# A graph layer's turn table: attention 21 turns sooner, 256-node blocks from node 4096

## The reference

```
msg = relu(x[src] + edge_attr @ w_e + b_e)                # gather of 131072 rows
agg = segment_sum(msg, dst, 8192)
h_local = bn1(relu((x + agg) @ w1 + b1) @ w2 + b2 + x)
q, k, v = split(x.reshape(256, 32, 256) @ in_w.T + in_b)  # attention inside 32 nodes, 4 heads
h_attn = bn2(softmax(q k^T / 8) v @ out_w.T + out_b + x)
out = h_local + h_attn
out = bn3(out + relu(out @ m_w1 + m_b1) @ m_w2 + m_b2)
return layernorm(x + out)
```

## Time and profile before

| | us |
|---|---|
| median of 3 runs | 1297.24 (1296.2 to 1297.25) |
| the profiled execution | 1296.03 |
| its span, first to last instruction | 1294.2 |
| busy: PE / DVE / ACT / POOL | 1154.5 / 826.7 / 541.2 / 944.9 |
| mean granted TensorE clock | 0.969 of full speed |

### The profile page before, as it was taken

The page is one execution under the profiler, slowest core; times in us unless marked ns, Lnnn a source line. Parts: engine busy times, 40 slices in busy tenths (PEclk is TensorE's granted clock), DMA queues, the critical chain, the costliest instruction groups (busy, mean ns, idle before and its releaser), DMA issues.

```text
span 1294.2 us, 28246 instructions
## 1 busy us (share of the span) xinstructions
PE 1154.5 (89%) x7309; PEld 647.4 (50%) x7309; DVE 826.7 (64%) x2090; ACT 541.2 (42%) x1077; POOL 944.9 (73%) x1004
## 2 busy tenths in 40 slices
PE   6787989998899899998989999998989998998896
PEld 3444454544445444444544545454444555765675
DVE  5847486767566576755758666575756667557563
ACT  1343434444344435434344443443434443443353
POOL 7777777777777777777777777777777777675770
PEclk7898999999999999999999999999999998999999
DMA  8554555655555555565555555555655565554550
GB/s 316 154 170 141 175 156 175 174 173 180 170 165 169 164 182 172 160 183 148 183 173 175 165 165 176 166 175 174 172 164 154 183 183 147 168 160 126 175 155 26
DMA packets 119282, 216.50 MB, mean 167 GB/s; under 512 B 24784, under 2 KB 69584, under 8 KB 119120
## 3 DMA queue, kind: packets, MB, share of 16 engines
q0 software_dynamic: 47808, 130.61, 35.0%
q1 hardware_dynamic: 67312, 79.47, 19.6%
q10 hardware_dynamic: 4000, 4.61, 1.0%
HBM read 197.82 MB, written 16.78 MB: 166 GB/s over the span
## 4 chain that ended last, share of the span: by engine, by line
PE 58%; DVE 11%; ACTq 8%; ACT 7%; issue 7%; POOL 6%; DMA 2%; DVEq 0%; SPq 0%
PE bank L837 33%; PE bank L867 12%; PE bank L882 7%; POOL xg L430 6%; ACTq L463 6%; ACT msg L469 4%; DVE bank L681 3%; PE bank L891 3%; ACTq L311 2%; DVE dif L731 2%; DVE mx L726 2%; PE bank L938 1%; DMA xT<-in_xT_dram 1%; DVE aggT L714 1%; ACT kbd L490 1%
## 5 line engine op out<-in xcount | busy, mean ns | idle before, releaser
L430 POOL DMA_INDIRECT xg<-in_x_dram,srcs x996 | 944.0, 948 | 317.4 <-issue 290.0
L469 ACT ACTIVATE msg<-bank 128x512 f32<-128x512 f32 x512 | 277.8, 595 | 543.6 <-PE bank L867 286.7
L681 DVE TENSOR_TENSOR bank<-xg,bank 128x512 f32<-128x512 f32 x498 | 327.4, 690 | 138.1 <-DMA xg<-in_x_dram,srcs 93.0
L867 PE MATMUL bank<-we,ea 64*128 64x256 f32 x2048 | 301.7, 415 | 35.5 <-DVE bank L681 35.5
L867 PEld LDWEIGHTS bank<-we,ea 64*128 64x128 f32 x2048 | 183.1, 192 | 179.7 <-issue 124.1
L714 DVE TENSOR_TENSOR aggT<-bank,aggT 128x64 f32 x512 | 115.2, 225 | 169.1 <-PE bank L891 115.2
L882 PE MATMUL bank<-msg,onehot 128*32 128x256 f32 x2048 | 141.1, 394 | 49.0 <-ACT msg L469 48.4
L837 PE MATMUL bank<-xT,iwT 128*128 128x512 f32 x256 | 128.2, 624 | 7.6 <-DMA xT<-in_xT_dram 4.0
L837 PE MATMUL bank<-o,m 128*128 128x512 f32 (+2 forms) x352 | 125.6, 491 | 4.6 <-DVE o L758 4.4
L882 PEld LDWEIGHTS bank<-msg,onehot 128*32 128x32 f32 x2048 | 54.4, 111 | 141.6 <-ACT msg L469 96.9
L837 PE MATMUL bank<-h,m 128*128 128x512 f32 (+2 forms) x352 | 116.6, 479 | 2.1 <-ACT h L529 2.1
(11 more groups left out here) (92 smaller groups left out, 938.9 us busy)
## 6 DMA issues: line engine op xcount, KB each, us to landing
rows<-in_x_dram SPq DMA_DIRECT2D x2304, 1.0 KB
ea<-in_ea_dram SPq DMA_DIRECT2D x128, 256.0 KB
rows<-in_x_dram ACTq DMA_DIRECT2D x1280, 1.0 KB
xg<-in_x_dram,srcs POOLq DMA_INDIRECT x996
xT<-in_xT_dram SPq DMA_DIRECT2D x32, 256.0 KB, 4.2
aggT<-in_xT_dram SPq DMA_DIRECT2D x32, 256.0 KB, 4.0
oT_dram<-oT SPq DMA_DIRECT2D x32, 256.0 KB
xn<-in_x_dram SPq DMA_DIRECT2D x32, 256.0 KB
```

Of the source, the lines that this page charges most:

```text
L430: pool.indirect_dma_start(xg[:, slot % NX, n * C:(n + 1) * C], None, t["x"], bass.IndirectOffsetOnAxis(k.srcs[:, at:at + 1], 0)).then_inc( ...
L469: nc.scalar.activation(msg[:, q % NM, :], EA[q % 4][:, :], ACT.Relu).then_inc(s_msg, 1)
L681: nc.vector.tensor_tensor(EA[q % 4][:, :].rearrange("p (a c) -> p a c", a=2), pair.rearrange("p (a c) -> p a c", a=2), KB[:, 0:C].unsqueez ...
L867: ins = nc.tensor.matmul(EA[(2 * d + pair) % 4][:, two * C:(two + 1) * C], ea[rows, n % NEA, at:at + P], k.we[rows, :], start=False, stop= ...
```

## The change

Attention starts its slabs at turns 0, 7, 14, 21 with a plan of seven turns, and from slab 4 at 16 J - 33 with a wider plan; before, it was 12 J for the first slabs and then 16 J - 12. `xT` has four slots instead of three, `oT` three instead of two, and the messages have four slots instead of eight. Blocks of 512 nodes end at node 4096 instead of 6144; fourteen blocks of 256 follow instead of six. SyncE loads x for the attention at other turns. From turn 254 on TensorE's order is written out by hand, and the attention's half of step B of the last two 128-node blocks becomes a step of its own, "A".

```
--- before.py
+++ after.py
@@ -26,7 +26,7 @@
 ND = NP // 2
 NB = N // IT
 NX = 7
-NM = 8
+NM = 4
 NEA = 3
 AHEAD = 3
 SLACK = 1
@@ -45,7 +45,7 @@
     0, 6, 8, 10, 12, 14, 16, 18, 20, 24, 26, 28)
 NV = 30
 
-NXT, NOT = 3, 2
+NXT, NOT = 4, 3
 
 ROWS, LOADED = 2 * P, 16
 SP_ROWS, SP_TURNS, SP_LEAD = 9, 242, 9
@@ -53,33 +53,36 @@
 SCALE_TURN, FOLD_TURN, BIAS_TURN = 9, 11, 12
 
 
-HEADS = {"q": (0, 1), "k": (2, 3), "sc": (4, 6), "soft": (5, 7), "v": (8, 9), "av": (11, 13)}
-HEADS_EARLY = {"q": (0, 1), "k": (2, 3), "sc": (4, 5), "soft": (5, 6), "v": (7, 8), "av": (9, 10)}
+HEADS = {"q": (0, 2), "k": (3, 5), "sc": (6, 8), "soft": (7, 9), "v": (10, 11), "av": (13, 14)}
+HEADS_EARLY = {"q": (0, 0), "k": (1, 1), "sc": (2, 3), "soft": (3, 4), "v": (4, 4), "av": (5, 6)}
+EARLY = 4
 
 
 def heads_base(J):
-    return max(16 * J - 12, 12 * J)
-
-
-
-BLOCKS = [(FULL * J, FULL) for J in range(12)] + [
-    (6144 + 256 * n, 256) for n in range(6)] + [(7680 + 128 * n, 128) for n in range(4)]
+    return 7 * J if J < EARLY else 16 * J - 33
+
+
+
+BLOCKS = [(FULL * J, FULL) for J in range(8)] + [
+    (4096 + 256 * n, 256) for n in range(14)] + [(7680 + 128 * n, 128) for n in range(4)]
 NODES = {"w1": (0, 1), "B": (3, 5), "z": (4, 6), "m1": (7, 8, 9, 10), "m2": (11, 13),
          "T": (14, 15), "log": (15, 16), "y": (16, 17), "xn": (8, 9), "out": (17, 18)}
 NODES_256 = {"w1": (0,), "B": (1,), "z": (2,), "m1": (2, 3), "m2": (4,), "T": (5,), "log": (6,),
              "y": (7,), "xn": (2,), "out": (8,)}
-FIRST_256 = {12: 211, 13: 217, 14: 223, 15: 229, 16: 235, 17: 243}
+FIRST_256 = dict(enumerate(
+    (147, 154, 161, 168, 175, 182, 189, 196, 203, 211, 219, 227, 235, 243), 8))
 NODES_128 = {
-    18: {"w1": (247,), "B": (248,), "z": (249,), "m1": (249,), "m2": (250,), "T": (251,),
+    22: {"w1": (247,), "B": (248,), "z": (249,), "m1": (249,), "m2": (250,), "T": (251,),
          "log": (252,), "y": (253,), "xn": (247,), "out": (254,)},
-    19: {"w1": (250,), "B": (251,), "z": (252,), "m1": (252,), "m2": (253,), "T": (254,),
-         "log": (255,), "y": (256,), "xn": (), "out": (257,)},
-    20: {"w1": (254,), "B": (255,), "z": (256,), "m1": (256,), "m2": (257,), "T": (258,),
-         "log": (259,), "y": (260,), "xn": (252,), "out": (261,)},
-    21: {"w1": (256,), "B": (257,), "z": (258,), "m1": (258,), "m2": (259,), "T": (260,),
-         "log": (260,), "y": (261,), "xn": (), "out": (262,)},
+    23: {"w1": (250,), "B": (251,), "z": (252,), "m1": (252,), "m2": (253,), "T": (254,),
+         "log": (256,), "y": (257,), "xn": (), "out": (258,)},
+    24: {"w1": (255,), "B": (256,), "z": (256,), "m1": (257,), "m2": (258,), "T": (260,),
+         "log": (260,), "y": (261,), "xn": (252,), "out": (262,)},
+    25: {"w1": (256,), "B": (257,), "z": (257,), "m1": (258,), "m2": (259,), "T": (260,),
+         "log": (260,), "y": (262,), "xn": (), "out": (263,)},
 }
-LASTB = 21
+LAST_TURN = 254
+LASTB = 25
 
 
 SUMS = {2 * n + 1: n for n in range(NG)}
...
...
...
@@ -366,10 +369,10 @@
                     load_ea(turn // 2 + 2)
                 if p == 3 and i + AHEAD < IT:
                     preload(i + AHEAD)
-                if turn in (2, 12):
-                    load_xT(1 if turn == 2 else 2)
-                if turn % 16 == 13 and NXT <= (turn + 19) // 16 < NJ:
-                    load_xT((turn + 19) // 16)
+                if turn in (1, 7, 13):
+                    load_xT((turn + 5) // 6)
+                if turn % 16 == 10 and NXT <= (turn + 38) // 16 < NJ:
+                    load_xT((turn + 38) // 16)
                 for J, _, pair in heads_in(turn - 1, ("av",)):
                     sp.wait_ge(s_oc, 2 * J + pair + 1)
                     sp.dma_start(k.oT_dram[2 * J + pair, :, :, :],
...
@@ -969,7 +972,7 @@
 
             def node(b, stage, use):
                 n0, w = BLOCKS[b]
-                at, to = cols(b), bank(b, stage)
+                at, to = cols(b), bank(b, "B" if stage == "A" else stage)
                 J, of_slab = part(b)
                 if stage == "w1":
                     if use:
@@ -978,9 +981,9 @@
                         if b == 0:
                             pe.wait_ge(s_w1, 16)
                             pe.wait_ge(s_bias, 1)
-                        elif b < 18:
+                        elif b < 22:
                             pe.wait_ge(s_r, before(b, "T"))
-                        elif b == 18:
+                        elif b == 22:
                             pe.wait_ge(s_oc, 2 * NJ)
                         elif b < LASTB:
                             pe.wait_ge(s_r, before(b - 1, "T"))
@@ -989,18 +992,21 @@
                         ins = product(to[:, of], CC, lambda a: k.w1[:, a, c * P:(c + 1) * P],
                                       lambda a: aggT[:, a, n0:n0 + w])
                     ins.then_inc(s_p1, 1)
+                if stage == "A":
+                    pe.wait_ge(s_oc, 2 * NJ)
+                    if b < LASTB:
+                        pe.wait_ge(s_h1, before(b + 1, "w1"))
+                    for c, of in chunks(b, "B", use):
+                        product(bank(b, "B")[:, of], CC,
+                                lambda a: k.owT[:, a, c * P:(c + 1) * P],
+                                lambda a: k.oT[:, J % NOT, a, of_slab], start=c == 0,
+                                stop=False, skip=True)
                 if stage == "B":
-                    early = b == LASTB
+                    early = b >= 24
                     if use:
                         pe.wait_ge(s_o, before(b, "B") + use)
                     else:
                         pe.wait_ge(s_oc, (n0 + w + NB - 1) // NB)
-                    if early:
-                        for c, of in chunks(b, "B", use):
-                            product(to[:, of], CC, lambda a: k.owT[:, a, c * P:(c + 1) * P],
-                                    lambda a: k.oT[:, J % NOT, a, of_slab], start=c == 0,
-                                    stop=False, skip=True)
-                    if not use:
                         pe.wait_ge(s_h1, before(b + 1, "w1"))
                     for c, of in chunks(b, "B", use):
                         if not early:
@@ -1039,9 +1045,8 @@
                                                       k.z[:, c, row:row + P], ident[:, :])
                     ins.then_inc(s_t, 1)
 
-            for turn in range(TURNS):
-                if turn < ND:
-                    products(turn)
+            for turn in range(LAST_TURN):
+                products(turn)
                 if turn - 1 in SUMS:
                     transpose_agg(SUMS[turn - 1])
                 weights(turn)
@@ -1051,6 +1056,25 @@
                     node(b, stage, use)
                 if turn in SUMS:
                     sum_group(SUMS[turn])
+
+            products(ND - 2)
+            transpose_agg(NG - 2)
+            node(23, "T", 0)
+            products(ND - 1)
+            node(24, "w1", 0)
+            sum_group(NG - 1)
+            node(24, "A", 0)
+            transpose_agg(NG - 1)
+            node(24, "B", 0)
+            node(LASTB, "A", 0)
+            node(LASTB, "w1", 0)
+            node(24, "m1", 0)
+            node(LASTB, "B", 0)
+            node(LASTB, "m1", 0)
+            node(24, "m2", 0)
+            node(LASTB, "m2", 0)
+            node(24, "T", 0)
+            node(LASTB, "T", 0)
             with pe.If(pe.value_load(k.bad_i[0:1, 0:1], min_val=0, max_val=1) > 0):
                 pe.wait_ge(s_go, 1)
                 general_tensor(nc, k, g, pe)
```

More of the change, by code:

```diff
@@ L127, in nodes_in @@
     for b in range(len(BLOCKS)):
-        if b < 12:
+        if b < 8:
             plan, base = NODES, 16 * b + 19
-        elif b < 18:
+        elif b < 22:
             plan, base = NODES_256, FIRST_256[b]
@@ L140, in heads_in @@
     for J in range(NJ):
-        plan = HEADS_EARLY if J < 3 else HEADS
+        plan = HEADS_EARLY if J < EARLY else HEADS
         found += [(J, s, n) for s in stages for n, at in enumerate(plan[s])
@@ L297, in bank @@
                 return EA[("w1", "B", "m1", "m2", "T").index(stage) % 4]
-            return k.XA if b in (18, 20) else k.XN
+            return k.XA if b in (22, 24) else k.XN
         x_bytes = t["x"].rearrange("(a n) c -> a (n c)", a=1).bitcast(u8)
@@ L401, in stored @@
                 for n in range(NOT):
-                    sp.wait_ge(s_ost[n], 16 * (IT // NOT))
+                    sp.wait_ge(s_ost[n], 32 * len(range(n, NJ, NOT)))
             with sp.If(sp.value_load(k.bad_i[0:1, 0:1], min_val=0, max_val=1) > 0):
```

## The result

The changed kernel takes 1343.25 us in the median (1341.27 to 1344.72), the kernel before 1297.24 beside it: a ratio of 1.035, 95% interval 1.0328 to 1.0372. The direction was right and the size was off by 30 us, beyond the range. The profiled execution has a span of 1342.2 us, 48.0 more than before.

The account below looks back on a forecast made before the run. The prediction took GpSimd's gathers to bound the kernel: 1296.0 + 29 (early slabs) - 10.3 (late stall) - 2.7 (end) = 1312 us, and 1313 as the runs' median lies 1.2 higher; range 1288 to 1326.

Parts of the forecast that it names:

- The gathers as the clock: Whole kernel: GpSimd's 996 gathers set the pace, 5.01 us per turn of four; other work matters only by delaying them.
- the first rival: Early turns: the backlog fits in the three-turn gather ring, no early stall, 1284 us; chance 0.20.
- The late stall, 10.3 us to gain: Late turns: 11.3 us of gather stalls, from turn 211's six-turn 'quick stretch' with attention in it, shrink to 1 us.
- The early slabs, 29 us: First four attention slabs: each takes about 40 us where seven turns of gathers give 35.1; 29 us lost.
- that falls here, 1.0: Early slabs: allowance of 1.0 us per slab for TensorE running slower after a long wait.
- seven turns being too few for 40 us: Early slabs: a slab's handshakes need about 40 us, while GpSimd needs 35.1 us for seven turns.
- Behind that, slabs come 16 turns apart as today and need less than the gathers give: After the early slabs: attention at the old spacing causes no further gather stall.
- TensorE's columns are the same: nothing while the gathers set the pace: Eight more 256-wide blocks: double VectorE and ScalarE instructions for four slabs fit in idle time, costing nothing.
- 1 us of stall left: Denser blocks and late turns: stall remaining after the change, between bounds of nothing and 11.3 us.
- The third rival: Turns 147 to 221: denser blocks stall five attention slabs, 15 us on top, 1328 us; chance 0.07.
- Slots and moved loads at nothing: Message slots and SyncE's x loads: no cost; about 5 us of SyncE's time if slab 12's load loses its cover.
- The end, -2.7, order worth 0: Last turns: without attention the products follow the last gather sooner, saving 2.7 us; the written-out order adds nothing.

Follow-up runs that it names:

- Run 2: Kernel before with the changed kernel's attention turns and slots, blocks and end as before: 1327.5 us, ratio 1.0251.
- run 1: Changed kernel with attention's turns and x loads of the kernel before: 1309.3 us, ratio 1.011.
- Run 16: Kernel before with written-out end and all nodes to 7680 in 256-wide blocks, mostly eight turns apart from turn 15: 1288.5 us, ratio 0.9941.
- run 7: Kernel before with written-out end, changed slots, four early slabs nine turns apart on the tight plan, later slabs 16 turns sooner: 1313.5 us, ratio 1.0109.
- run 12: Kernel before with its three early slabs, 12 turns apart, on the changed kernel's tight early plan: 1315.4 us, ratio 1.0135.
- run 10: Kernel before with written-out end, changed slots, four spread early slabs nine turns apart, but both q in one turn and both k in one: 1312.8 us, ratio 1.0106.
- run 5: Kernel before with written-out end, changed slots, four early slabs seven turns apart on the tight plan, old later plan 16 turns sooner: 1322.1 us, ratio 1.0188.
- run 3: Kernel before with only the slots changed (four message, four x, three output): 1295.5 us, ratio 0.9988.
- run 15: Kernel before with written-out end and 256-wide blocks from node 4096, starting at turn 151, eight, later six turns apart: 1313.7 us, ratio 1.0136.
- run 8: Kernel before with written-out end, changed slots, four early slabs nine turns apart, q, k and scores spread over turns 0 to 5: 1295.0 us, ratio 0.9972.

## Why the prediction was wrong, step by step

- **The gathers as the clock**: right. The added time is waits for seeds. As to the first rival, its stall-free start did not come: 996 gathers of 947 ns took 48 us more. The rule of the Trainium skill (Perfetto Trace Analysis, What "DMA-bound" means), by which a kernel is bound on the issuing sequencer where its track is solid with DMA slices, names the bound here but not what holds it up.
- **The late stall, 10.3 us to gain**: right, 11.1. Run 2 gains 9.9 with the old blocks, run 1 nothing with the new: attention's leaving did it, as argued. Run 16 gets the same by having no quick stretch. I had put the stall down to VectorE's softmax, but TensorE itself had no room there: in turns 211 to 226 its rows without the waits take 81.0 us before and 70.4 in the changed kernel, where GpSimd gives 80. In the wait of the earlier trace rows VectorE was at the scores' differences and at a block's normalising.
- **The early slabs, 29 us**: right in kind, too small in size. The slabs took 46.2, 41.0 and 47.1 us (from 63.53 to 109.70, 150.74 and 197.85 above), forecast 42, 41.7 and 45.3. Run 2, with the same early instructions, took 43.1, 40.8 and 45.4, began the products of turns 7, 14, 21 and 28 within 0.7 us of the forecast (60.4, 103.5, 144.4, 189.8), and lost 28.6; its profiled execution is the fastest of its four. The mis-sized term is "that falls here, 1.0" for a slower TensorE. From turn 7 to turn 14 TensorE waited 10.6 us and worked 35.5 in the changed kernel, and waited 10.3 and worked 32.8 in run 2. In turn 11 the two v steps stand behind nearly the same waits in both; the second took 3.78 us in the changed kernel, where the mean granted clock was 0.59, and 1.99 in run 2 at 1.00 (changed kernel, run 2, and their windows):

```profile
92.31 2.75 PE L840 MATMUL bank<-iwT,xT 128*128 128x256 f32 x8 [1.79 <-DVE dif L734]
95.74 3.78 PE L840 MATMUL bank<-iwT,xT 128*128 128x256 f32 x8 [0.68 <-ACT qT L504]
```

```profile
89.05 1.99 PE L838 MATMUL bank<-iwT,xT 128*128 128x256 f32 x8 [1.53 <-DVE dif L732]
91.72 1.99 PE L838 MATMUL bank<-iwT,xT 128*128 128x256 f32 x8 [0.68 <-ACT qT L502]
```

```profile
92.00:100.00 8.00, 7.01 (x24) 4.59 (x28) 7.44 (x26) 1.44 (x3) 2.86 (x4) 0.59 0.42 111
```

```profile
86.00:94.00 8.00, 5.79 (x38) 4.25 (x38) 7.66 (x21) 2.33 (x5) 2.43 (x3) 1.00 0.30 82
```

  7.6 us are missing here. At turn 28 the changed kernel is 8.1 us behind run 2, 3.1 of them from before turn 7. Where I read the cost as seven turns being too few for 40 us, runs 7 and 12 show that more turns do not take it away, and run 10 shows the doubled q and k as the larger part.
- **"Behind that, slabs come 16 turns apart as today and need less than the gathers give"**: failed, 9.1 us. The same spacing with another plan is not the same load. ScalarE's messages of turns 114 to 117 stand behind row fetches, six at a time; the groups' sums of turns 115 and 117 wait for messages, and the products after them take 2.08 us instead of 1.13 (ScalarE's timeline, then TensorE's; the granted clock is 0.68 to 0.84 from 620 to 650 us):

```profile
617.16 3.46 ACTq L466 DMA_DIRECT2D rows<-in_x_dram  x6
620.67 1.08 ACT L472 ACTIVATE msg<-bank 128x512 f32<-128x512 f32 x2 [3.20 <-issue]
...
635.47 3.73 ACTq L466 DMA_DIRECT2D rows<-in_x_dram  x6
639.25 1.08 ACT L472 ACTIVATE msg<-bank 128x512 f32<-128x512 f32 x2 [3.16 <-issue]
```

```profile
626.47 1.94 PE L885 MATMUL bank<-msg,onehot 128*32 128x256 f32 x16 [2.88 <-ACT msg L472]
628.34 2.08 PE L870 MATMUL bank<-we,ea 64*128 64x256 f32 x8
...
640.38 1.93 PE L885 MATMUL bank<-msg,onehot 128*32 128x256 f32 x16 [2.93 <-ACT msg L472]
```

  It came in both profiles of the changed kernel and in run 2, at the same turns (9.1, 9.0, 8.9). That the shifted plan does it is shown by run 5; that the row fetches have a part in it is only read from the timeline.
- **"TensorE's columns are the same: nothing while the gathers set the pace"** for the 256-wide blocks, with 1 us of stall left: this step failed most, 18.8 us. The columns are the same and their place is not. I had weighed VectorE's 40.7 us of waiting as room; TensorE's work, 69 to 71 of 80 us in each 16 turns of the kernel before from 147 to 210 (its rows without the waits between them), was the room to look at, and its heaviest four turns. The third rival named the stretch and nearly the price (15), but gave it a chance of 0.07.
- **Slots and moved loads at nothing**: right for the slots (run 3). Of the moved loads, SyncE waited 15.8 us at one between 800 and 900 us, where I had about 5, and TensorE then 1.7 us for edge attributes; run 15 shows what such a load costs without its cover.
- **The end, -2.7, order worth 0**: the tail shrank by 5.4, and the written-out order alone gives 3.8, attention's absence alone 1.3. The term that I took as nothing was the larger.

Sum of the misses: 7.6 + 9.1 + 18.0 (blocks and late turns together 7.7 instead of -10.3) - 2.7 = 32.0, which is 48.0 less the 16.0 forecast for the span.

## What to carry to other kernels

Where several engines walk a table of turns, add up the busiest engine's work turn by turn, not per period: a form with the same columns in fewer, heavier turns stalls where it meets another stage's heavy turns, and two turns of shift decided it here (1343 against 1288 us). Don't put two steps through one bank into one turn to save turns: with everything else the same, that cost 18 us here (runs 8 and 10), by the waits and the slower clock behind them. Before moving work into a stretch with slack, see how fast a backlog shrinks there (0.9 to 1.5 us a turn here).

## What the runs showed of the hardware

A step of eight v products took 1.99 us at a granted clock of 1.00 (run 2) and 3.78 where the window's mean was 0.59 (changed kernel). The Trainium skill (TensorE: Matmul & The Clock Gate, Part 1) says that the array's clock has two levels, 1.2 and 2.4 GHz, and that activity releases the throttle; the two times agree with two levels. The same waits did not always bring the lower one: behind waits of 1.53 and 0.68 us both v steps of run 2 took 1.99, while the changed kernel, run again, took 3.50 and 1.99 behind the same two. Kernels with the same early instructions differed by up to 8 us by turn 44 (28.6 to 36.6). Six row fetches held ScalarE's queue for 2.09 us at 609 us of the changed kernel's span and for 3.46 eight us later.
